# Shared expert tiles load tokens transposed in the attention phase; ScalarE's order within a tile

## The chip, the cores and the metric

The kernel runs on one core of a Trainium2 chip. The metric is device time in microseconds (us) of one execution of the whole program, lower is better. A core has TensorE (PE in the profile), VectorE (DVE), ScalarE (ACT), GpSimd (POOL) and SyncE (SP). They run side by side and wait for each other on semaphores; SP, ACT and POOL also issue DMA transfers.

## The reference

4096 tokens of width 1024 pass through a cross-attention-like product and then through a mixture of experts; each is added to its input:

```python
x = x + einsum("emk,enk->emn", fp8_blocks(layernorm(x)), fp8_blocks(ctx))
h = layernorm(x)                                   # T = 4096 tokens, H = 1024
scores = sigmoid(h @ gate_w)                       # 32 experts; 6 are chosen per token
expert_out = sum_k weight_k * (silu(h @ w_gate[e_k]) * (h @ w_up[e_k])) @ w_down[e_k]   # inner width 704
shared = (silu(h @ sw_gate) * (h @ sw_up)) @ sw_down                                    # inner width 1408
out = x + expert_out + shared
```

## The kernel before

Tokens are handled in tiles of 128. The 4096 tokens are TT = 32 tiles, and the whole program has three stages.

**Attention phase.** For each of the 32 tiles all engines work in a hand-written software pipeline (`beside` of each engine). At its end the normalised tokens of tile i, split into a high and a low float16 part, lie in `x2nat` (128 tokens x 2 x 1024). SP stores them to the DRAM tensor `rows_x` (`store_x2`, L319). TensorE also transposes them into PSUM (`ps_t`), and ScalarE copies them to `xT`, half u = 0 of `xT_pair` (`take_x2`), for the product with the router's matrix (`logits`). SP's loop holds, in order: store of x1, load of the residual, store of x2, load of x for tile i+4, load of ctx for tile i+11. In the last nine tiles parts of the shared expert's weights are loaded too.

**Tiles.** Then follows one loop of tiles, numbered n. Tiles 0 to 31 are all tokens through the first half of the shared expert (704 of its 1408 inner columns). Tiles 32 on are routed tiles: each is 128 token rows of one expert. Here there are 208 of them (tiles 32 to 239), and `n_tiles` is 240. The last 32 tiles are all tokens through the second half of the shared expert. During the first shared pass GpSimd scatters the token rows into the experts' slots in `rows_x` (six indirect DMAs of 512 KB per token tile), and SP loads those tiles for it and writes zeros. During the last pass GpSimd gathers six rows of results per token from `rows_d`, and VectorE adds them (`combine`).

TensorE does, for tile n: gate and up (`gate_up`, 72 matmuls into `ps_gu`), then the down product of tile n-1 (34 matmuls into `ps_d`). The weights are two buffers of an expert each, which GpSimd converts from float32. Before gate and up of tile n it waits for the tokens (`xt_in`) and for `hid` of tile n-1 (`hid_done`), since `ps_gu` is one buffer; before the down product it waits for the transposed hidden values (`ht_in`, tile hT) and for `d_free`.

**ScalarE, per tile** (function `tile`): wait for gate and up of tile n; issue the DMA transposition of the tokens of tile n+2 from `xin` into half u of `xT_pair` (`turn_x`, L907); `silu` (L914); copy VectorE's `hid` to float16 (L920); issue the transposition of the hidden values, `hT` (`turn_h`, L931), once VectorE has written their low part; wait until the tokens of n+2 have landed (`xin_free`) and load those of n+3 into `xin`, which is one buffer (`load_x`, L902); empty `ps_d` of tile n-1 into `dout` (`store_d`, L936) and store that to `rows_d` (L938). In the last shared pass `store_d` is left out, and VectorE takes `ps_d` itself. All of ScalarE's DMAs stand in one queue (q10), all of SP's in another (q1), GpSimd's in a third (q0).

Of the kernel before, what the change touches and what calls it, by code (L numbers as in the profile page):

```python
# [22 lines left out]
F16 = mybir.dt.float16  # L23
# [5 lines left out]
ds = bass.ds  # L29

P = 128
B, S, H = 4, 1024, 1024
# [5 lines left out]
T = B * S  # L38
TT = T // P
# [49 lines left out]
def build(nc, x, ctx_in, gate_w, w_gate, w_up, w_down, sw_gate, sw_up, sw_down, out):  # L89
# [4 lines left out]

    rows_x = nc.dram_tensor("rows_x", (T + SLOT_TILES * P, 2 * H), F16).ap()
    rows_d = nc.dram_tensor("rows_d", (T + SLOT_TILES * P, H), F32).ap()
    rows_x1 = nc.dram_tensor("rows_x1", (T, H), F32).ap()
    last_row = T + SLOT_TILES * P - 1

    with ExitStack() as stack:  # L100
# [6 lines left out]
        def sem(name):  # L107
            return stack.enter_context(nc.semaphore(name))
# [5 lines left out]
        xT_pair = sb("xT", [P, 2, 2 * KH, P], F16)  # L114
# [66 lines left out]
        def pair(area, i):  # L181
# [40 lines left out]
            for n in ("qin_in", "qin_free", "rounded", "unrounded", "deq_ready", "nat_high", "nat_ready"))  # L222
# [13 lines left out]
            sem(n) for n in ("route_step", "top_ready", "sig_ready", "mask_ready", "rank_done", "rank_used",  # L236
                             "slots_ready", "tables_ready", "pad_out"))

        xin_in, xt_in, gu_done, silu_done = (sem(n) for n in ("xin_in", "xt_in", "gu_done", "silu_done"))
        hid_done, hid_high, hid_low, ht_in, down_done, d_free, d_out = (sem(n) for n in (  # L240
            "hid_done", "hid_high", "hid_low", "ht_in", "down_done", "d_free", "d_out"))
# [11 lines left out]
        X, CTX = 0, 1  # L253
# [21 lines left out]
        def set_of_x2(i):  # L275
            return X_SETS - TT + i if isinstance(i, int) and i >= TT - 2 else i * 2 + 3
# [7 lines left out]
        def _(sp):  # L284
# [20 lines left out]
            def load_q(kind, i):  # L305
                sp.wait_ge(qin_free[kind], i + 1)
                sp.dma_start(qin[kind], (x_rows, c_rows)[kind][ds(i * P, P), :]).then_inc(qin_in[kind], 16)
# [9 lines left out]
            def store_x2(i):  # L317
                sp.wait_ge(x2_ready, i + 2)
                sp.dma_start(rows_x[ds(i * P, P), :], x2nat.rearrange("p a d -> p (a d)")).then_inc(x2_out, 16)  # L319

            load_q(CTX, 0)
            load_q(X, 0)
            load_res(0)
# [10 lines left out]
            def stores(i):  # L334
                store_x1(i)
                if not isinstance(i, int) or i < TT - 1:
                    load_res(i + 1)
                store_x2(i)

            with sp.Fori(0, TT - CLEAD - 1) as i:  # L340
                stores(i)
                load_q(X, i + (LEAD + 1))
                load_q(CTX, i + (CLEAD + 1))
            with sp.Fori(TT - CLEAD - 1, TT - CLEAD + 1) as i:
                stores(i)
                load_q(X, i + (LEAD + 1))
            for i in range(TT - CLEAD + 1, TT):
                stores(i)
                if i < TT - LEAD - 1:
                    load_q(X, i + (LEAD + 1))  # L350
                c = STAGES + i - (TT - CLEAD + 1)
                sp.wait_ge(conv_done, c - STAGES + 1)
                load_piece(0, c, *half_a)

            for c in range(STAGES + CLEAD - 1, CHUNKS):
                sp.wait_ge(conv_done, c - STAGES + 1)
                load_piece(0, c, *half_a)
# [431 lines left out]
        def _(act):  # L789
# [9 lines left out]
            def take(high, low, ps):  # L799
                for half, to in enumerate((high, low)):  # L800
                    last = a.activation(to, ps[:, half, :].rearrange("p (k n) -> p k n", k=KH), ACT.Copy)
                return last
# [9 lines left out]

            def take_x2(i):
                act.wait_ge(tr_done, set_of_x2(i) + 1)
                take(xT[:, 0], xT[:, 1], ps_t).then_inc(tr_free, 1)

            def high_of_nat(kind, i):
# [83 lines left out]
            def load_x(n, row):  # L901
                act.dma_start(xin[:, :, :].rearrange("p a d -> p (a d)"), rows_x[ds(row, P), :]).then_inc(xin_in, 16)  # L902

            def turn_x(n, u):
                act.wait_ge(xin_in, n * 16 + 16)
                act.sem_inc(act_turn, 1)
                act.dma_start_transpose(xT_pair[:, u, :, :],  # L907
                                        xin[:, :, :].rearrange("p a d -> p (a d)")).then_inc(xt_in, 16)

            def xin_free(n):  # L910
                act.wait_ge(xt_in, n * 16 + 16)
# [13 lines left out]
            def turn_h(n, u, used=True):  # L925
                act.wait_ge(hid_high, n + 1)
                act.wait_ge(hid_low, n + 1)
                if used:
                    act.wait_ge(down_done, n if n is n_tiles else n - 1)
                act.sem_inc(act_turn, 1)  # L930
                act.dma_start_transpose(hT[:, u, :, :], hid_hl[:, :]).then_inc(ht_in, 16)  # L931
# [5 lines left out]
                act.wait_ge(d_free, n + 2)  # L937
                act.dma_start(rows_d[ds(n * P, P), :], dout[:, :]).then_inc(d_out, 16)  # L938

            def tile(n, u, next_row=None, first=False, turn=True, used=True, store=True):  # L940

                act.wait_ge(gu_done, n + 1)
                if turn:
                    turn_x(n + 2, u)
                silu(n)
                high_of_hidden(n, first)
                turn_h(n, u, used)
                if next_row is not None:
                    xin_free(n + 2)
                    load_x(n + 3, next_row)  # L950
                if store:
                    store_d(n - 1)

            act.wait_ge(x2_out, 16 * TT + 16)
            load_x(0, 0)
            act.wait_ge(logits_done, TT)
            turn_x(0, 0)
            xin_free(0)
            load_x(1, P)
            turn_x(1, 1)  # L960
            xin_free(1)
            load_x(2, 2 * P)
            tile(0, 0, 3 * P, first=True, used=False, store=False)
            tile(1, 1, 4 * P, used=False)
            with act.Fori(1, TT // 2 - 2) as q:
                for u in range(2):
                    tile(q * 2 + u, u, (q * 2 + (u + 3)) * P)
            tile(TT - 4, 0, (TT - 1) * P)

            act.wait_ge(tables_ready, 1)  # L970
            act.wait_ge(pad_out, 16 * E)
            for u in range(2):
                act.wait_ge(scat_out[u], 16 * TOPK * TT // 2)
            tile(TT - 3, 1, TT * P)
            with act.Fori(TT // 2 - 1, N_ALL // 2 - 2) as q:
                for u in range(2):
                    tile(q * 2 + u, u, (q * 2 + (u + 3)) * P)
            tile(N_ALL - 4, 0, (N_ALL - 1) * P)
            n_tiles = act.value_load(count_tab[0:1, 0:1], min_val=N_ALL, max_val=N_MAX)
            act.wait_ge(zeros_out, 16 * (EXTRA + 1))  # L980

            def late(n, u):
                row = act.value_load(row_tab[0:1, ds(n - (N_ALL - 3), 1)], min_val=0, max_val=N_MAX - 1)
                tile(n, u, row * P)

            late(N_ALL - 3, 1)
            late(N_ALL - 2, 0)
# [3 lines left out]
                    for u in range(2):  # L991
                        late(q * 2 + u, u)

            tile(n_tiles, 0, 3 * P)
            tile(n_tiles + 1, 1, 4 * P, store=False)
            with act.Fori(1, TT // 2 - 2) as q:
                for u in range(2):
                    tile(n_tiles + (q * 2 + u), u, (q * 2 + (u + 3)) * P, store=False)
            tile(n_tiles + (TT - 4), 0, (TT - 1) * P, store=False)
            tile(n_tiles + (TT - 3), 1, store=False)  # L1000
            for u in range(2):
                tile(n_tiles + (TT - 2 + u), u, turn=False, store=False)


        @block.vector
# [380 lines left out]
```

## Time and profile before

| | us |
|---|---|
| median of three runs | 7482.79 |
| lowest and highest | 7464.86, 7521.01 |
| the profiled execution, its own time | 7488.26 |
| its span | 7486.6 |
| busy in it: TensorE | 6540.5 (87%) |
| busy: GpSimd | 3376.8 (45%) |
| busy: VectorE | 1598.3 (21%) |
| busy: ScalarE | 1032.4 (14%) |

The page gives shares over the whole span; the stages have different limits, so they are to be read one by one. A DMA share is the mean busy share of the core's 16 DMA engines, and can go over 1 where transfers overlap on an engine. PEclk is TensorE's granted clock, 1.00 being 2.4 GHz.

### The profile page before, as it was taken

What the parts mean: (1) busy time and instruction counts of PE and PEld (TensorE: products, weight loads), DVE (VectorE), ACT (ScalarE), POOL (GpSimd) and SP (SyncE); (2) the same over time, 40 slices, a digit from 0 to 9 for tenths busy, and PEclk for the clock granted to TensorE, in tenths of its full rate; (3) what the DMA queues carried; (4) which work ended last, traced back from release to release, by engine and by line L of the source; (5) the groups of instructions that cost most, each with busy time, mean ns of one, the idle gap of its engine ahead of it and who ended that gap; (6) DMA issues with size and microseconds to landing.
All of it is one profiled execution on the core that took longest, in us unless ns stands there. A gap on an engine that the chain in (4) does not pass through costs nothing.

```text
span 7486.6 us, 89283 instructions
## 1 busy us (share of the span) xinstructions
PE 6540.5 (87%) x32678; PEld 3097.2 (41%) x32679; DVE 1598.3 (21%) x2586; ACT 1032.4 (14%) x1206; POOL 3376.8 (45%) x2190
## 2 busy tenths in 40 slices
PE   1455568768999999999999999999999999988878
PEld 0233333323444444444444444444444444433333
DVE  3555582000011101111110111111011111124435
ACT  1333330000111111111111111111111111100000
POOL 3555584434055336534543564553554545512222
PEclk9777779889999999999999999999999999999989
DMA  1222237997355555555555565555565555567897
GB/s 50 75 84 85 90 128 235 334 294 209 92 154 160 139 138 158 160 141 141 158 153 137 150 170 140 155 162 136 155 168 141 158 154 155 153 191 219 220 199 219
DMA packets 1270964, 1190.42 MB, mean 159 GB/s; under 512 B 995728, under 2 KB 995728, under 8 KB 1270928
## 3 DMA queue, kind: packets, MB, share of 16 engines
q10 hardware_dynamic: 1031168, 509.19, 29.8%
q1 hardware_dynamic: 179856, 471.02, 19.7%
q0 software_dynamic: 59904, 209.75, 8.1%
q8 instruction: 20, 0.33, 0.0%
q14 instruction: 16, 0.13, 0.0%
HBM read 647.10 MB, written 310.38 MB: 128 GB/s over the span
## 4 chain that ended last, share of the span: by engine, by line
PE 73%; DMA 8%; issue 7%; ACTq 5%; POOL 4%; DVE 3%; ACT 1%; SPq 0%; POOLq 0%; DVEq 0%
PE ps_gu L623 50%; PE ps_d L623 20%; ACTq L907 4%; DMA xT<-xin 3%; DMA xin<-rows_x 3%; POOL wts L474 2%; PE ps_d L726 2%; DMA wts<-in_x 2%; PE ps_d L724 1%; ACTq L931 1%; POOL wts L479 1%; DMA hT<-hid_hl 1%; POOL wts L465 0%; DVE hid L1218 0%; DVE amax_p L1032 0%
## 5 line engine op out<-in xcount | busy, mean ns | idle before, releaser
L623 PE MATMUL ps_gu<-wts,xT 128*128 128x512 f16 (+1 forms) x19584 | 3988.4, 366 | 206.5 <-DVE hid L1218 199.2
L623 PEld LDWEIGHTS ps_gu<-wts,xT 128*128 128x128 f16 x19584 | 1908.3, 99 | 2284.6 <-issue 398.4
L623 PE MATMUL ps_d<-wts,hT 128*128 128x512 f16 x8160 | 1829.1, 383 | 119.8 <-DMA hT<-hid_hl 119.3
L449 POOL TENSOR_SCALAR wts<-stage 128x1408 f16<-128x1408 f32 (+1 forms) x476 | 588.5, 1236 | 2422.7 <-PE ps_d L726 2406.2
L1218 DVE SCALAR_TENSOR_TENSOR hid<-ps_gu,sil 128x704 f32<-128x704 f32 x272 | 242.4, 891 | 5083.5 <-ACT sil L914 5083.5
L452 POOL TENSOR_TENSOR wts<-stage,wts 128x1408 f16<-128x1408 f32 (+1 forms) x476 | 1248.2, 2622 | 39.8
L623 PEld LDWEIGHTS ps_d<-wts,hT 128*128 128x128 f16 x8160 | 802.1, 98 | 1090.2 <-DMA hT<-hid_hl 116.3
L914 ACT ACTIVATE sil<-ps_gu 128x704 f32<-128x704 f32 x272 | 205.9, 757 | 4261.6 <-issue 4193.7
L450 POOL TENSOR_SCALAR stage<-stage 128x1408 f32<-128x1408 f32 (+1 forms) x476 | 610.2, 1282 | 0.0
L614 PE MATMUL ps_t<-ident,wts 128*128 128x128 f16 x1024 | 89.0, 257 | 366.2 <-POOL wts L474 361.6
L623 PE MATMUL ps_d<-wts,xin 128*128 128x512 f16 x1536 | 367.6, 399 | 42.4 <-DVE wts L1112 33.0
L936 ACT ACTIVATE dout<-ps_d 128x1024 f32<-128x1024 f32 x240 | 245.6, 1024 | 1088.6 <-issue 530.0
L589 POOL COPY slot_now<-slot 128x6 int32 (+1 forms) x32 | 6.0, 186 | 644.8 <-DVE wts L1250 572.8
L474 POOL TENSOR_TENSOR wts<-wts 128x1024 f16<-128x1024 f32 x64 | 173.7, 2726 | 240.9 <-issue 213.7
L1225 DVE TENSOR_TENSOR hid_hl<-hid,hid_hl 128x640 f16<-128x640 f32 x272 | 265.1, 974 | 0.0
L920 ACT ACTIVATE hid_hl<-hid 128x704 f16<-128x704 f32 x272 | 214.8, 790 | 281.8 <-DVE hid L1218 281.8
L1250 DVE SCALAR_TENSOR_TENSOR wts<-wts,top_w 128x1024 f32<-128x1024 f32 x192 | 246.6, 1284 | 26.4 <-DVE wts L1247 3.6
L623 PEld LDWEIGHTS ps_d<-wts,xin 128*128 128x128 f16 x1536 | 153.2, 102 | 231.7 <-issue 41.5
L614 PEld LDWEIGHTS ps_t<-ident,wts 128*128 128x128 f16 x1024 | 79.1, 117 | 387.1 <-issue 329.0
L594 POOL DMA_INDIRECT wts<-rows_d,slot_now x192 | 192.8, 1004 | 76.9 <-issue 48.8
L553 POOL DMA_INDIRECT rows_x<-wts,slot_now x192 | 186.7, 973 | 78.0 <-issue 49.6
L614 PE MATMUL ps_gu<-ident,wts 128*128 128x128 f16 x512 | 56.3, 299 | 155.3 <-POOL wts L474 155.3
(149 smaller groups left out, 2230.7 us busy)
## 6 DMA issues: line engine op xcount, KB each, us to landing
xin<-rows_x ACTq DMA_DIRECT2D x272, 512.0 KB, 4.0
rows_d<-dout ACTq DMA_DIRECT2D x240, 512.0 KB
stage<-in_L_ffn_w_down SPq DMA_DIRECT2D x384, 256.0 KB, 3.1
stage<-in_L_ffn_w_gate SPq DMA_DIRECT2D x256, 352.0 KB, 3.7
stage<-in_L_ffn_w_up SPq DMA_DIRECT2D x256, 352.0 KB, 4.2
wts<-in_x SPq DMA_DIRECT2D x64, 512.0 KB, 5.6
rows_x<-wts SPq DMA_DIRECT2D x64, 512.0 KB, 3.3
wts<-rows_x SPq DMA_DIRECT2D x64, 512.0 KB, 7.3
```

Of the source, the lines that this page charges most:

```text
L449: g.tensor_scalar(high, raw, WSCALE, 1.0, ALU.mult, ALU.mult).then_inc(conv_step, 1)
L450: g.tensor_scalar(raw, raw, WSCALE, 1.0, ALU.mult, ALU.mult).then_inc(conv_step, 1)
L452: g.tensor_tensor(low, raw, high, ALU.subtract).then_inc(conv_done, 1)
L474: g.tensor_tensor(nat[kind][:, 1, :], deq[kind], nat[kind][:, 0, :], ALU.subtract)\
L614: last = nc.tensor.transpose(to[:, a, k * P:(k + 1) * P], src[:, a, k * P:(k + 1) * P], ident[:, :])
L623: ins = nc.tensor.matmul(dst[c], left, right[c], start=(first and a == 0), stop=(last and a == 2))
L907: act.dma_start_transpose(xT_pair[:, u, :, :], xin[:, :, :].rearrange("p a d -> p (a d)")).then_inc(xt_in, 16)
L920: a.activation(hid_hl[:, 0:M], hid[:, :, :].rearrange("p a c -> p (a c)"), ACT.Copy)\
L936: a.activation(dout[:, :], ps_d_flat, ACT.Copy, scale=1.0 / (WSCALE * HSCALE)).then_inc(d_free, 1)
L1218: v.scalar_tensor_tensor(out=hid[:, :, :].rearrange("p a c -> p (a c)"), in0=ps_gu_flat[:, M:2 * M], scalar=HSCALE / WSCALE, in1=sil[:, :, ...
L1225: v.tensor_tensor(hid_hl[:, M + M_LAST:], flat[:, 0:K_LAST], hid_hl[:, 0:K_LAST], ALU.subtract).then_inc(hid_low, 1)
L1250: ins = v.scalar_tensor_tensor(out=total[u], in0=gat[u][:, k, :], scalar=top_w[:, ds(i, 1), k:k + 1].rearrange("p a k -> p (a k)"), in1=to ...
```

## The change

A new DRAM tensor `cols_x` holds the tokens of each tile in the layout of `xT`. In the attention phase SP stores `xT` of tile i-1 into it once ScalarE has copied it there (`store_xt`), and ScalarE waits for the store of the tile before ahead of the next copy (`take_x2`). In both shared passes ScalarE loads the tokens of tile n+2 from `cols_x` with one plain DMA (`load_t`); `xin` and its transposition remain for the routed tiles. The order in `tile` becomes: `silu`, high part of the hidden values, `turn_h`, then the next tokens (`load_t`, or `turn_x` and `load_x`), then `store_d`.

```diff
+    cols_x = nc.dram_tensor("cols_x", (T, 2 * H), F16).ap()
...
+            def store_xt(i):
+                sp.wait_ge(tr_free, set_of_x2(i) + 2)
+                sp.dma_start(cols_x[ds(i * P, P), :], xT_pair[:, 0, :, :].rearrange("p k n -> p (k n)")).then_inc(xt_out, 16)
...
-            with sp.Fori(0, TT - CLEAD - 1) as i:
+            stores(0)
+            load_q(X, LEAD + 1)
+            load_q(CTX, CLEAD + 1)
+            with sp.Fori(1, TT - CLEAD - 1) as i:
                 stores(i)
                 load_q(X, i + (LEAD + 1))
                 load_q(CTX, i + (CLEAD + 1))
+                store_xt(i - 1)
             with sp.Fori(TT - CLEAD - 1, TT - CLEAD + 1) as i:
                 stores(i)
                 load_q(X, i + (LEAD + 1))
+                store_xt(i - 1)
             for i in range(TT - CLEAD + 1, TT):
                 stores(i)
+                store_xt(i - 1)
                 if i < TT - LEAD - 1:
                     load_q(X, i + (LEAD + 1))
                 c = STAGES + i - (TT - CLEAD + 1)
                 sp.wait_ge(conv_done, c - STAGES + 1)
                 load_piece(0, c, *half_a)
 
+            store_xt(TT - 1)
...
             def take_x2(i):
                 act.wait_ge(tr_done, set_of_x2(i) + 1)
+                if not isinstance(i, int) or i > 0:
+                    act.wait_ge(xt_out, i * 16)
+                    act.sem_inc(act_turn, 1)
                 take(xT[:, 0], xT[:, 1], ps_t).then_inc(tr_free, 1)
...
             def turn_x(n, u):
-                act.wait_ge(xin_in, n * 16 + 16)
+                act.wait_ge(xin_in, (n - TT) * 16 + 16)
...
+            def load_t(n, i, u):
+                if not isinstance(n, int) or n > 0:
+                    act.wait_ge(xt_in, n * 16)
+                act.dma_start(xT_pair[:, u, :, :].rearrange("p k n -> p (k n)"),
+                              cols_x[ds(i * P, P), :]).then_inc(xt_in, 16)
...
-            def tile(n, u, next_row=None, first=False, turn=True, used=True, store=True):
+            def tile(n, u, next_row=None, next_cols=None, first=False, turn=False, used=True, store=True, fresh=False):
 
                 act.wait_ge(gu_done, n + 1)
-                if turn:
-                    turn_x(n + 2, u)
                 silu(n)
                 high_of_hidden(n, first)
                 turn_h(n, u, used)
+                if next_cols is not None:
+                    load_t(n + 2, next_cols, u)
+                if turn:
+                    turn_x(n + 2, u)
                 if next_row is not None:
-                    xin_free(n + 2)
+                    if not fresh:
+                        xin_free(n + 2)
                     load_x(n + 3, next_row)
                 if store:
                     store_d(n - 1)
 
-            act.wait_ge(x2_out, 16 * TT + 16)
-            load_x(0, 0)
+            act.wait_ge(xt_out, 16 * TT)
             act.wait_ge(logits_done, TT)
-            turn_x(0, 0)
-            xin_free(0)
-            load_x(1, P)
-            turn_x(1, 1)
-            xin_free(1)
-            load_x(2, 2 * P)
-            tile(0, 0, 3 * P, first=True, used=False, store=False)
-            tile(1, 1, 4 * P, used=False)
+            load_t(0, 0, 0)
+            load_t(1, 1, 1)
+            tile(0, 0, next_cols=2, first=True, used=False, store=False)
+            tile(1, 1, next_cols=3, used=False)
             with act.Fori(1, TT // 2 - 2) as q:
                 for u in range(2):
-                    tile(q * 2 + u, u, (q * 2 + (u + 3)) * P)
-            tile(TT - 4, 0, (TT - 1) * P)
+                    tile(q * 2 + u, u, next_cols=q * 2 + (u + 2))
+            tile(TT - 4, 0, next_cols=TT - 2)
...
-            tile(TT - 3, 1, TT * P)
+            tile(TT - 3, 1, TT * P, next_cols=TT - 1, fresh=True)
```

The routed tiles get `turn=True` and are called as before; the calls of the last shared pass get `next_cols` in place of a row.

## Rows read from the trace of the kernel before

**Rows 1.** The chain that ended last, on the page: shares of the span by line.

```profile
PE ps_gu L623 50%; PE ps_d L623 20%; ACTq L907 4%; DMA xT<-xin 3%; DMA xin<-rows_x 3%; POOL wts L474 2%; PE ps_d L726 2%; DMA wts<-in_x 2%; PE ps_d L724 1%; ACTq L931 1%; POOL wts L479 1%; DMA hT<-hid_hl 1%; POOL wts L465 0%; DVE hid L1218 0%; DVE amax_p L1032 0%
```

**Rows 2.** Line 914 in three windows: count, ns min/median/max, first and last start.

```profile
L914 ACT ACTIVATE sil<-ps_gu x18: 757/757/757, 1214.7 to 1787.3; 128x704 f32<-128x704 f32 x18
...
L914 ACT ACTIVATE sil<-ps_gu x220: 757/757/761, 1787.3 to 6562.6; 128x704 f32<-128x704 f32 x110
...
L914 ACT ACTIVATE sil<-ps_gu x32: 757/757/757, 6591.1 to 7446.2; 128x704 f32<-128x704 f32 x32
```

**Rows 3.** Windows: length; busy PE, PEld, DVE, ACT, POOL; PEclk, DMA share, GB/s.

```profile
1214.70:1787.30 572.60, 409.43 (x1803) 182.01 (x1801) 31.64 (x51) 43.69 (x51) 230.12 (x247) 0.85 1.06 303
1787.30:6588.60 4801.30, 4797.99 (x23312) 2241.95 (x23311) 512.81 (x660) 565.47 (x660) 2299.84 (x1369) 1.00 0.55 149
6588.60:7446.10 857.50, 718.30 (x3288) 326.22 (x3287) 359.81 (x333) 48.98 (x63) 194.27 (x220) 0.92 0.82 220
```

**Rows 4.** Waits of PE, 1214.7 to 1787.4: total us, times, longest us.

```profile
PE ps_gu L623 <- DVE hid L1218: 93.4, 13, 16.5
PE ps_d L623 <- DMA hT<-hid_hl: 69.2, 7, 18.3
```

**Rows 5.** Waits of PE, 6588.6 to 7446.3.

```profile
PE ps_gu L623 <- DVE hid L1218: 98.7, 21, 10.2
PE ps_d L623 <- DMA hT<-hid_hl: 40.5, 5, 16.4
```

**Rows 6.** Timeline of ACT in a routed tile: start, length, engine, line, operation.

```profile
3028.47 1.88 ACTq L907 DMA_TRANSPOSE xT<-xin  x1
...
3034.07 1.39 ACTq L931 DMA_TRANSPOSE hT<-hid_hl  x1
...
3036.43 1.02 ACT L936 ACTIVATE dout<-ps_d 128x1024 f32<-128x1024 f32 x1 [3.45 <-PE ps_d L726]
```

**Rows 7.** Timeline of ACT, tile 15; in brackets idle before and releaser.

```profile
1600.97 21.39 ACTq L931 DMA_TRANSPOSE hT<-hid_hl  x1
...
1624.55 1.02 ACT L936 ACTIVATE dout<-ps_d 128x1024 f32<-128x1024 f32 x1 [24.66 <-DMA xT<-xin]
```

**Rows 8.** Timeline of PE, the down product of the same tile.

```profile
1631.84 7.94 PE L623 MATMUL ps_d<-wts,hT 128*128 128x512 f16 x30 [18.30 <-DMA hT<-hid_hl]
```

**Rows 9.** Timeline of ACT, tile 0: the turn's issue.

```profile
1145.24 3.77 ACTq L907 DMA_TRANSPOSE xT<-xin  x1
```

**Rows 10.** DMA issues, 1214.7 to 1787.4: count, KB each, median us to landing.

```profile
xin<-rows_x ACTq DMA_DIRECT2D x17, 512.0 KB, 9.3
...
xT<-xin ACTq DMA_TRANSPOSE x17, 20.1
```

**Rows 11.** DMA issues, 6588.6 to 7446.3.

```profile
xin<-rows_x ACTq DMA_DIRECT2D x29, 512.0 KB, 4.0
...
xT<-xin ACTq DMA_TRANSPOSE x30, 14.4
```

**Rows 12.** Timeline of the last tile: hT's issue and its use.

```profile
7449.79 4.60 ACTq L931 DMA_TRANSPOSE hT<-hid_hl  x1
...
7463.14 8.97 PE L623 MATMUL ps_d<-wts,hT 128*128 128x512 f16 x30 [9.54 <-DMA hT<-hid_hl]
```

**Rows 13.** Timeline of SP's queue in the attention phase.

```profile
592.25 0.45 SPq L307 DMA_DIRECT2D wts<-in_ctx  x1
...
1084.86 0.34 SPq L319 DMA_DIRECT2D rows_x<-wts  x1
```

**Rows 14.** DMA issues, 300 to 900, attention phase.

```profile
wts<-in_ctx SPq DMA_DIRECT2D x19, 512.0 KB, 6.2
```

**Rows 15.** Timeline of ACT: xT copies of a steady step and of tile 31.

```profile
604.07 1.91 ACT L801 ACTIVATE xT<-ps_t 128x1024 f16<-128x1024 f16 x2
...
1086.81 1.94 ACT L801 ACTIVATE xT<-ps_t 128x1024 f16<-128x1024 f16 x2 [4.18 <-PE ps_t L614]
```

**Rows 16.** Timeline of POOL: its last operation on the first routed expert's weights.

```profile
1823.87 2.13 POOL L452 TENSOR_TENSOR wts<-stage,wts 128x1024 f16<-128x1024 f32 x1
```

## What I predict

> **What bounds the kernel now.** I read the page's chain first: TensorE's two products hold 70% of it, but a transposition's issue on ScalarE's queue, the transpositions `xT<-xin` and the loads `xin<-rows_x` hold 10% more [rows 1]. The next question is in which stage. The counts of `silu` give the stages in tiles [rows 2]: tile 3 at 1214.7 us, tile 20 at 1787.3, tile 239 at 6562.6, and 32 more, the second shared pass, up to 7446.2. The 219 steps of the middle take 4775.3 us, 21.81 us each, and TensorE is busy in 4798.0 of 4801.3 us there at full clock [rows 3]: that is the time of a tile when nothing disturbs it. Against it the two shared passes are slow:
>
> - Tiles 3 to 20, while GpSimd scatters the rows and the DMA share is 1.06: 572.6 us for 17 steps, 33.7 each. At 21.81 they would be 370.7, so 201.9 us are lost. TensorE was idle for 572.6 - 409.4 = 163.2 of them; the other 38.7 are matmuls at a granted clock of 0.85 [rows 3].
> - The second shared pass, while GpSimd gathers, DMA share 0.82: 857.5 us for 31 steps, 27.7 each. At 21.81 that is 676.1, so 181.4 are lost: 139.2 idle, 42.2 clock [rows 3].
>
> Together 383 us are there to be had. TensorE's waits say on what it idles: on `hid` 93.4 us in 13 waits and on `hT` 69.2 in 7 [rows 4]; in the second pass on `hid` 98.7 in 21 and on `hT` 40.5 in 5 [rows 5]. `hid` itself is cheap. In a quiet tile ScalarE issues xT's transposition (1.88 us), `silu` follows, and hT is issued 5.60 us after the start of the turn [rows 6]; TensorE has the down product of the tile before to do meanwhile and sees nothing of it. In the crowded stretches the issue of a transposition takes up to 21.39 us [rows 7] and xT's stands ahead of `silu`: gate and up of the next tile wait for `hid`. hT is then queued behind xT, and the down product waits for it: issued at 1600.97, used at 1631.84, 30.9 us later [rows 7, 8]. ScalarE also stands 24.66 us before it empties `ps_d`, because `xin_free` waits for xT to land [rows 7]. xin is a single buffer: load, turn, load follow each other whatever TensorE does.
>
> **The change, part by part.** *First tile.* The issue of 3.77 us stood between the product and `silu` with TensorE idle [rows 9]; it goes: 3.8 us gained.
>
> *Shared tiles, order.* `silu` and the copy come first, then hT is issued: by the quiet tile 5.60 - 1.88 = 3.7 us after the product ends. The slow issue can no longer delay `hid`, so the waits on it of 93.4 and 98.7 us go, unless ScalarE is late for another reason: after hT it has one plain load to issue and, in the first pass, `dout` to make and store, due 21.8 us after the product.
>
> *Shared tiles, transfers.* xT's 16 blocks of 128x128 per tile are no longer transposed, hT's 11 are. A plain load of the same 512 KB landed in 9.3 us where the transposition took 20.1 [rows 10]. The wait in `xin_free`, and the turn that depends on a load, go too. So what is late next is hT alone. It may take 21.8 - 3.7 = 18.1 us. Its price with nothing of xT ahead is seen once, in the last tile with a gather running: issued at 7449.79, used at 7463.14, 13.4 us [rows 12]. In the scatter stretch xT's 20.1 scaled by 11/16 gives 13.8. Both fit into 18.1; the tail doesn't, the late one above took 30.9 with xT ahead. I take one tile in three of the scatter stretch 4 us late, with 2 us of slow clock behind each stall (38.7 / 17 = 2.3 per tile now): 2.0 us a tile. In the gather stretch, where transposition and load land in 14.4 and 4.0 us [rows 11], I take 0.8. Bounds: nothing, and on the other side 6 us in each tile of the first and 3 in each of the second (hT at about 22 us in every tile of the first pass, between 13.8 and 30.9).
>
> Of the 572.6 us I keep 490 as crowded (the last step is quiet already, and the scatter should end some 50 us sooner with the small packets gone; 50 us more or less are only 50 x 2.0 / 23.8 = 4 us of the sum). 490 / 23.8 = 20.6 tiles, 41 us lost instead of 201.9: 161 gained. In the second pass 31 x 0.8 = 25 us instead of 181.4: 156 gained. VectorE, which combines there, is busy 359.8 / 31 = 11.6 us a tile [rows 3] and is no new bound.
>
> The Trainium skill (Advanced Engine Details and Errata, X-Bar Transpose) says that on trn2 a transposing DMA is as fast as a regular one. In the scatter stretch it isn't: 20.1 against 9.3 us [rows 10]. By the rule only one of two equal passes over the tokens would be saved, and I would halve the part of the gain that comes from transfers.
>
> *Routed tiles.* Nothing is removed; the turn moves behind hT. xT then lands behind hT's issue at 3.7 us, two issues of 1.4 and 1.9 us and both transfers, at about 11 us (estimate: 3.7 + 3.3 + 4). ScalarE stands in `xin_free` until then; queued behind it are the next load and `dout`, which starts at 7.96 us now [rows 6] and would at about 12. TensorE needs `ps_d` at 21.8, so there are 9 us of cover: cost 0.
>
> *Attention phase.* A store of 512 KB per tile goes on SP's queue. In a steady step it follows the load of ctx, issued at 592.25, so near 592.7 [rows 13]. That load lands 6.2 us after its issue [rows 14], the store then near 600; ScalarE's new wait stands ahead of the xT copies at 604.07 [rows 15]. 4 us of cover, 0 paid. In five of the last nine steps the store stands ahead of the load of x: 0.5 us on each, 2.5. At the very end it is seen: the store of tile 30 goes out behind the one at 1084.86 [rows 13], lands near 1090 (estimate, a little under the 6.2), and the copy of tile 31 starts now at 1086.81 [rows 15]: 3.3 us on the path to the routing. Together 6 (bounds 0 and 20, the latter one us in each of twenty steps).
>
> *The first routed weights.* Tile 23.6 would be at 1214.7 + 490 = 1705 and tile 31 at 1866; tile 32's product follows the down product. GpSimd ends its last part of these weights at 1826 [rows 16]: 40 us of cover, 0 paid, unless the scatter ends that much later than now.
>
> Sum: 7486.6 - 3.8 - 161 - 156 + 6 = 7172 of span. The profiled execution took 7488.3, 1.7 more than its span and 5.5 more than the median shown, so against the median 7168; I say **7170 us**.
>
> **Rivals.** *(a) hT takes the place of both.* It moves slowly among scatter and stage traffic even with nothing ahead of it, because of its many small packets. At the bounds above: 490 / 27.8 = 17.6 tiles x 6 = 106 and 31 x 3 = 93 us lost, so 383.3 + 3.8 - 199 - 6 = 182 gained, 7301 us. For it: seven waits on hT, up to 18.3 us [rows 4]. Against: xT was ahead in all of them, and the 13.4 us seen alone [rows 12]. The Trainium skill (DMA: Bandwidth & Descriptors, Queues, rings and completion order) has each DMA engine go round between its queues packet by packet; that rule speaks for this rival, as small packets would then give way to large ones as often.
>
> *(b) No change.* The DMA engines are full, they stay full, and what is left waits as long as before; within 1%. Against: in the second pass their share is 0.82 [rows 3], so there is room, and the `hid` waits are of order, not of bytes.
>
> *(c) Slower: the routed tiles.* If xT behind hT lands after some 20 us, `dout` comes too late and each of the 208 routed tiles stretches. The point is 9 us beyond my 11; 1.5 us a tile beyond that eat the whole gain, and 2 give 416 - 315 = +101, 7584 us. Against: at the middle's DMA share of 0.55 [rows 3] ScalarE's plain loads land in 4 us or so, as they do at 0.82 [rows 11].
>
> **How the numbers follow.** Forecast 0.74, (a) 0.18, (b) 0.04, (c) 0.04. The forecast's own range is 7115 (both stretches nearly clean) to 7260. The range reaches up to (a): 7110 to 7300. Over 1% is about what can be told from no change here. Faster than that are the forecast, (a) and a little of the rest: 0.93; same 0.03; slower 0.04.
>
> **What would show it.** In the changed profile: steps of `silu` of 23 to 24 us in the scatter stretch and near 22.6 in the second pass; waits on `hid` all but gone, those on hT fewer but not zero; granted clock above 0.95 in both; full TensorE in the routed tiles; tile 3 at most 5 us later than now. Steps of 27 and 25 us with hT as the releaser would make (a) right. If `hid` is still waited for, the order was not the cause. Gaps ahead of the routed tiles' down products would be (c). A first product more than 20 us later would make my cost of the attention phase wrong.

## The result and the profile after

| | before | after |
|---|---|---|
| median, us | 7484.82 (4 runs) | 7118.26 (4 runs) |
| lowest and highest | 7464.86, 7521.01 | 7109.32, 7169.77 |
| ratio, with 95% interval | 1 | 0.9519 [0.9461, 0.9578] |
| span of the profiled execution | 7486.6 | 7113.4 |

The changed kernel is 4.8% faster. It was run again on another chip with some of the experiments below: 7126.09 us (7119.70 to 7140.62) against 7586.19 (7502.76 to 7629.47) for the kernel before there, 0.9425 [0.9354, 0.9496]. All ratios in this document leave out executions that took over 1.5% longer than the fastest of their kernel on that chip; medians and ranges hold them.

The lines of `silu` (L936 now; line numbers are those of the changed kernel) answer to [rows 2], in the same three parts, tiles 3 to 20, 20 to 239, 240 to 271:

```profile
L936 ACT ACTIVATE sil<-ps_gu x18: 757/757/757, 1202.8 to 1582.4; 128x704 f32<-128x704 f32 x18
...
L936 ACT ACTIVATE sil<-ps_gu x220: 757/757/757, 1582.4 to 6362.0; 128x704 f32<-128x704 f32 x110
...
L936 ACT ACTIVATE sil<-ps_gu x32: 757/757/757, 6388.8 to 7074.7; 128x704 f32<-128x704 f32 x32
```

The scatter stretch takes 379.6 us for its 17 steps (22.3 each, it was 33.7), the second pass 685.9 for 31 (22.1 each, it was 27.6 by this count). The middle has not moved. The windows with the same ends, to be read against [rows 3]:

```profile
1202.80:1582.40 379.60, 372.89 (x1803) 173.68 (x1802) 31.50 (x51) 43.67 (x51) 156.22 (x181) 1.00 1.01 328
1582.40:6362.00 4779.60, 4776.05 (x23216) 2234.41 (x23215) 532.12 (x657) 562.94 (x658) 2382.01 (x1441) 1.00 0.58 156
6388.80:7074.70 685.90, 678.15 (x3288) 316.62 (x3287) 361.97 (x333) 49.00 (x64) 201.25 (x220) 1.00 0.82 253
```

TensorE is idle 6.7 us in the first stretch (it was 163.2) and 7.8 in the last (139.2, in a window 2.4 us longer), and the granted clock is 1.00 in both. The DMA share has hardly moved, 1.01 and 0.82, but it now goes with 328 and 253 GB/s in place of 303 and 220. Waits of TensorE, first in the scatter stretch and then in the second pass; these are all that are left of [rows 4, 5], and none is on `hid`:

```profile
PE ps_d L636 <- DMA hT<-hid_hl: 6.7, 3, 2.4
...
PE ps_d L636 <- DMA hT<-hid_hl: 7.7, 2, 7.1
```

ScalarE in one tile of the scatter stretch, which answers to [rows 7]. hT's issue is still slow, but `silu` is ahead of it, and behind it stands a load of 1.60 us:

```profile
1337.85 0.76 ACT L936 ACTIVATE sil<-ps_gu 128x704 f32<-128x704 f32 x1 [12.82 <-PE ps_gu L636]
...
1341.52 6.70 ACTq L953 DMA_TRANSPOSE hT<-hid_hl  x1
1348.48 1.60 ACTq L929 DMA_DIRECT2D xT<-cols_x  x1
1350.21 1.02 ACT L958 ACTIVATE dout<-ps_d 128x1024 f32<-128x1024 f32 x1 [9.77 <-issue]
```

On the page's chain TensorE's two products are at 77% (70% in [rows 1]), and neither the transposition of the tokens nor their load is among its entries; hT's transposition is still there with 2%:

```profile
PE ps_gu L636 53%; PE ps_d L636 24%; POOL wts L487 2%; PE ps_d L739 2%; DMA hT<-hid_hl 2%; DMA wts<-in_x 2%; PE ps_d L737 2%; POOL wts L492 1%; POOL wts L478 0%; DVE amax_p L1050 0%; DVE stats_q L1108 0%; DVE wts L1284 0%; POOL wts L480 0%; SPq L321 0%; ACT wts L843 0%
```

### The profile page after: what moved, and what is told of

Its sections match the earlier page's. It is cut to its first block, busy times and chain, and to the rows that moved or that the text cites. A ratio compares the mean times of both kernels' runs of the same rounds, so it can differ in the third digit from the quotient of the medians.

```text
span 7113.4 us, 89519 instructions
## 1 busy us (share of the span) xinstructions
PE 6460.4 (91%) x32678; PEld 3079.8 (43%) x32679; DVE 1619.6 (23%) x2586; ACT 1032.1 (15%) x1206; POOL 3385.2 (48%) x2190
## 4 chain that ended last, share of the span: by engine, by line
PE 81%; issue 8%; DMA 4%; POOL 4%; DVE 3%; ACT 0%; SPq 0%; POOLq 0%; ACTq 0%; DVEq 0%
PE ps_gu L636 53%; PE ps_d L636 24%; POOL wts L487 2%; PE ps_d L739 2%; DMA hT<-hid_hl 2%; DMA wts<-in_x 2%; PE ps_d L737 2%; POOL wts L492 1%; POOL wts L478 0%; DVE amax_p L1050 0%; DVE stats_q L1108 0%; DVE wts L1284 0%; POOL wts L480 0%; SPq L321 0%; ACT wts L843 0%
## 5 line engine op out<-in xcount | busy, mean ns | idle before, releaser
L636 PE MATMUL ps_gu<-wts,xT 128*128 128x512 f16 (+1 forms) x19584 | 3929.7, 362 | 9.2 <-DVEq L1324 4.0
L636 PE MATMUL ps_d<-wts,hT 128*128 128x512 f16 x8160 | 1810.5, 380 | 26.8 <-DMA hT<-hid_hl 26.8
L465 POOL TENSOR_TENSOR wts<-stage,wts 128x1408 f16<-128x1408 f32 (+1 forms) x476 | 1232.2, 2589 | 39.8
L463 POOL TENSOR_SCALAR stage<-stage 128x1408 f32<-128x1408 f32 (+1 forms) x476 | 628.6, 1321 | 0.0
L936 ACT ACTIVATE sil<-ps_gu 128x704 f32<-128x704 f32 x272 | 205.9, 757 | 2844.8 <-PE ps_gu L636 2514.1
L636 PE MATMUL ps_d<-wts,xin 128*128 128x512 f16 x1536 | 368.7, 400 | 44.4 <-DVE wts L1130 34.2
L1243 DVE TENSOR_TENSOR hid_hl<-hid,hid_hl 128x640 f16<-128x640 f32 x272 | 299.6, 1102 | 0.0
```

The source lines that it names most:

```text
L463: g.tensor_scalar(raw, raw, WSCALE, 1.0, ALU.mult, ALU.mult).then_inc(conv_step, 1)
L465: g.tensor_tensor(low, raw, high, ALU.subtract).then_inc(conv_done, 1)
L636: ins = nc.tensor.matmul(dst[c], left, right[c], start=(first and a == 0), stop=(last and a == 2))
L936: a.activation(sil[:, :, :].rearrange("p a c -> p (a c)"), ps_gu_flat[:, 0:M], ACT.Silu, scale=1.0 / WSCALE).then_inc(silu_done, 1)
L1243: v.tensor_tensor(hid_hl[:, M + M_LAST:], flat[:, 0:K_LAST], hid_hl[:, 0:K_LAST], ALU.subtract).then_inc(hid_low, 1)
```

## The experiments

Two things were changed in the shared tiles at once: what is transferred (a plain load for load, turn and wait) and in which order ScalarE issues it. Theory A is that the transposition's traffic and the chain through xin were the cost, theory B that the slow issue ahead of `silu` was. Two kernels do one of the two each, which with the kernel before and the changed one makes a table of four.

### The order alone

```diff
# kernel before, tile()
-                if turn:
-                    turn_x(n + 2, u)
                 silu(n)
                 high_of_hidden(n, first)
                 turn_h(n, u, used)
+                if turn:
+                    turn_x(n + 2, u)
```

> The kernel before with one part of the change: silu, the high part and hT's issue come first in every tile, the turn of the next tokens after them; tokens still go through xin and are transposed in every tile. Theory A (the transposition and the single xin buffer are the cost): in the crowded stretches ScalarE's queue has to do hT (9.8 us), xT (20.1) and the load (9.3) one after the other, 39 us, so the steps of tiles 3 to 20 stay at 33 us or more; in the second shared pass 10.6 + 13.7 + 4.0 = 28, so steps near 28; the total stays above 7420 us. Theory B (the order is the cost, because a slow issue stood ahead of silu): steps of 22 to 24 us in both, total 7120 to 7180 us.

Measured: 7261.41 us (7254.95 to 7262.57), 0.9556 [0.9489, 0.9624]. Its windows, scatter stretch and second pass:

```profile
1206.10:1734.30 528.20, 402.19 (x1804) 179.32 (x1803) 31.49 (x51) 43.73 (x52) 208.02 (x240) 0.88 1.03 323
6538.50:7215.70 677.20, 676.28 (x3289) 316.29 (x3287) 362.08 (x333) 49.04 (x64) 201.97 (x220) 1.00 0.90 278
```

Neither theory has the total right (over 7420, and 7120 to 7180), because each fits one pass. In the second, theory B holds: the order alone takes all, 677.2 us, 21.8 per step, with every token tile still transposed. In the scatter stretch a step is 31.1 us, nearer to theory A's 33 than to B's 22 to 24, and the wait has moved. The waits of ScalarE and of TensorE there:

```profile
ACT dout L936 <- DMA xT<-xin: 443.5, 17, 39.3
...
PE ps_d L623 <- ACT dout L936: 120.4, 14, 22.9
```

Nothing waits for `hid` any more. ScalarE stands in `xin_free` before it may empty `ps_d`, and TensorE waits for that.

### The plain loads alone

```diff
# changed kernel, tile()
+                if next_cols is not None:
+                    load_t(n + 2, next_cols, u)
+                if turn:
+                    turn_x(n + 2, u)
                 silu(n)
                 high_of_hidden(n, first)
                 turn_h(n, u, used)
-                if next_cols is not None:
-                    load_t(n + 2, next_cols, u)
-                if turn:
-                    turn_x(n + 2, u)
```

> The changed kernel with the old order in every tile: the next tokens (plain load in shared tiles, turn in routed tiles) are issued ahead of silu. Theory A (transposition and xin are the cost): a plain load is issued in 0.4 to 1.6 us and puts only 128 rows ahead of hT; steps of 22 to 23 us in both shared passes, total 7118 to 7170 us. Theory B (the order is the cost): waits of TensorE on hid come back, steps of 27 us or more, total above 7300 us.

Measured: 7162.69 us (7120.72 to 7212.69), 0.9446 [0.9357, 0.9535].

```profile
1207.00:1595.40 388.40, 375.07 (x1804) 174.05 (x1803) 31.52 (x51) 43.74 (x52) 151.99 (x175) 0.98 1.03 314
6408.90:7084.50 675.60, 675.60 (x3286) 316.16 (x3285) 362.28 (x333) 49.01 (x64) 195.42 (x220) 1.00 0.78 257
```

22.8 us a step in the scatter stretch, 21.8 in the second pass: theory A's numbers in both. So in the first pass what is transferred gives nearly all of the gain without the order (184 of 193 us in the table), and the order without it does not (31.1 us a step). In the second, order and transfers each suffice, and neither may be credited with the gain by itself. "What is transferred" is still three things at once: the packets, the chain through xin, and the length of the issue, since a plain load is issued in a short time wherever it stands. Reckoned from profiled executions in us, for 17 and 31 steps:

| | scatter stretch | second pass |
|---|---|---|
| before, first chip | 572.6 | 855.1 |
| order alone | 528.2 | 677.2 |
| plain loads alone | 388.4 | 675.6 |
| both (the change), first chip | 379.6 | 685.9 |
| both, another chip | 384.4 | 686.5 |

The first column has to be read with care. The rows of order alone and of plain loads alone are from a chip on which the kernel before took 7516 to 7634 us and was not profiled. By the medians there the order alone is 336 us faster (7597.41 to 7261.41), while the table gives it 44.4 + 177.9. The difference is not located, and the scatter stretch also took 519.3 us in a kernel further down (less gather) that is the kernel before up to there. What the order alone gives in the scatter stretch is therefore not shown: somewhere from nothing to about 160 us. That 31.1 us a step are left with it, and 22.8 with the plain loads, is.

### The transposition's packets with nothing that depends on them

```diff
# changed kernel, tile(): 14 of xT's 16 blocks, zeros into a buffer that nobody reads
                 if next_cols is not None:
                     load_t(n + 2, next_cols, u)
+                    extra_turn(next_cols - 2 + extra_base[0])
...
+            def extra_turn(count):
+                if not isinstance(count, int) or count > 0:
+                    act.wait_ge(extra_in, count * 16)
+                act.sem_inc(act_turn, 1)
+                act.dma_start_transpose(spare_to[:, :, :], spare_from[:, :]).then_inc(extra_in, 16)
```

> The changed kernel, and in every shared tile that loads tokens ScalarE also issues, behind the plain load, a transposition of 14 blocks (xT has 16) from a buffer of zeros into a buffer that nobody reads; the only wait is for the one of the tile before. So the transposition's packets are back in the queue, but nothing depends on them: no bounce through xin, no xin_free, silu still first. If the packets themselves are the cost: hT has to go behind what is left of them, about 9.8 + 17.5 = 27 us in the scatter stretch and 10.6 + 12 = 23 in the second pass, steps of 28 to 33 us for tiles 3 to 20 and 24 to 27 in the second pass, total near 7400 us. If the chain load, turn, load and the waits on it are the cost: steps of 22 to 24 us, total below 7170 us.

Measured: 7373.38 us in one run. Windows as before:

```profile
1203.40:1806.50 603.10, 404.94 (x1804) 179.90 (x1803) 31.58 (x51) 43.71 (x51) 186.04 (x217) 0.83 1.10 251
6655.50:7331.60 676.10, 676.10 (x3288) 316.28 (x3286) 362.08 (x333) 48.98 (x64) 201.00 (x220) 1.00 0.89 277
```

In the scatter stretch the extra transposition alone brings the slow pass back, 35.5 us a step, with no chain through xin. The total is what was expected of the packets, but by other terms: the second pass does not suffer at all (24 to 27 us a step were expected), another 43 us stand in tiles 20 to 32 (308.2 against 265.6 in the change), where GpSimd issues its last scatter at 1875 in place of 1699, and in the scatter stretch TensorE hardly waits for hT. It waits for `dout`, which stands behind the issue of the extra transposition:

```profile
1513.48 19.96 ACTq L942 DMA_TRANSPOSE spare_to<-spare_from  x1
1533.57 1.02 ACT L970 ACTIVATE dout<-ps_d 128x1024 f32<-128x1024 f32 x1 [31.31 <-DMA xT<-cols_x]
...
PE ps_d L640 <- ACT dout L970: 185.8, 12, 23.7
...
PE ps_d L640 <- DMA hT<-hid_hl: 8.0, 2, 4.7
```

This edit also put the slow issue ahead of `dout`, so it shows that a second transposition per tile suffices for slow steps, and not whether by its packets or by its issue. The next kernel has `dout` ahead of everything slow.

### The turn behind everything

```diff
# kernel before, tile()
-                if turn:
-                    turn_x(n + 2, u)
                 silu(n)
                 high_of_hidden(n, first)
                 turn_h(n, u, used)
+                if store:
+                    store_d(n - 1)
+                if turn:
+                    turn_x(n + 2, u)
                 if next_row is not None:
                     xin_free(n + 2)
                     load_x(n + 3, next_row)
-                if store:
-                    store_d(n - 1)
```

> The kernel before with silu, hT and dout first in every tile and the turn and the load of the next tokens last; nothing is stored in the attention phase. In the order-only kernel TensorE's waits in the scatter stretch had moved to dout (120.4 us in 14 waits), which stood behind the wait for xT. If that place was all that was wrong, steps of 22 to 24 us for tiles 3 to 20 and a total near 7130 us: the stores and plain loads would not be needed. If the transposition's traffic is the cost there, ScalarE is then late for the next silu instead, because hT (15 us), turn (14 to 30) and load don't fit into 21.8: waits on hid or hT come back, steps of 27 us or more for tiles 3 to 20, total 7200 to 7300 us; the second pass is at 21.8 either way.

Measured: 7313.88 us (7279.63 to 7384.13), 0.9652 [0.9571, 0.9733]. In the profiled execution (span 7382.4, the upper end) the scatter stretch takes 656.5 us, 38.6 a step, at 260 GB/s and a share of 1.09; the second pass again 676.1. Waits of TensorE and of ScalarE in the stretch:

```profile
PE ps_gu L623 <- DVE hid L1218: 137.9, 12, 21.6
PE ps_d L623 <- DMA hT<-hid_hl: 91.0, 14, 11.7
...
ACT sil L914 <- DMA xT<-xin: 355.9, 11, 45.2
```

With the turn ahead of `silu` the wait is on `hid` and hT, behind hT it is on `dout`, behind `dout` it is on `hid` and hT again. None of the three places in ScalarE's queue helps in the scatter stretch. In the order-alone kernel it takes 20.4 us in the median from hT's issue to xT's last packet, and hT is issued 3.7 us after the product ends; with the turn last it takes 32.2. With the 3.7 us both are over the 21.8 us of a tile, and `xin_free` makes ScalarE wait for the end of it. Two things were not tried: a second xin buffer, with which ScalarE need not stand in `xin_free` (355.9 us ahead of `silu` above), and the turn on an engine other than ScalarE. How much of the cost is traffic and how much is this waiting stays open. From the packet records of ScalarE's queue, the time from an issue to the end of its last packet, median and longest, in us (order of the packets taken as that of the issues):

```
in us                     hT            xT
scatter stretch
before                  12.7, 29.5    20.1, 26.1
order alone             15.2, 27.8    13.7, 33.1
turn last               18.3, 23.7    25.3, 40.4
plain loads alone       11.8, 24.8    -
the change               9.8, 19.9    -

second pass
before                   3.1, 27.3    13.7, 29.2
order alone             10.5, 17.1     6.7, 14.7
the change              10.6, 22.0    -
```

The lower part shows why order alone is enough in the second pass. Before, the turn met the gather (13.7 us) while `silu` waited behind it, and hT came when the gather was over (3.1): in the 4 us after an issue the gather's packets fill 0.51 of the DMA engines' time in the median for xT and nothing for hT. With hT first, hT meets the gather (0.46) and takes 10.5 us, for which there are 18.1, and the turn comes behind it and takes 6.7.

### Less gather

```diff
# kernel before, gather() and combine()
-                for k in range(TOPK):
+                for k in range(1):
                     g.indirect_dma_start(
...
-                dve.wait_ge(gat_in[u], pair * (16 * TOPK) + 16 * TOPK)
+                dve.wait_ge(gat_in[u], pair * 16 + 16)
```

> The kernel before with one of the six gathers per tile in the last shared pass; VectorE still adds six rows, five of which are left-over data, so the output leaves out part of the routed experts' sum. Tokens are still transposed, ahead of silu. If the cost in the second pass is the meeting of the slow turn with the gather's traffic, the issue of the turn is short there again (1.4 to 2 us) and the steps are 21.8 to 22.5 us, 31 of them 676 to 697 us instead of 855. If the transposition or the order cost by themselves, steps stay at 27 us or more. The first shared pass is as slow as before in either case.

Measured: 7249.38 us in one run, beside 7516.76 for the kernel before. The second pass takes 683.4 us (first `silu` 6533.06, last 7216.49), 22.0 a step, and TensorE's waits on `hid` there are down from [rows 5]:

```profile
PE ps_gu L623 <- DVE hid L1218: 8.2, 10, 1.7
```

So neither order nor transposition costs anything there by itself. It takes the whole gather. The issue of the turn did not become as short as expected: 4.1 us in the median and up to 7.06, where 1.4 to 2 were expected and 9.5 was the median before. With issues of that length TensorE waits no more than the 8.2 us above.

### What the stores in the attention phase cost

```diff
# kernel before, with store_xt, its place on SP's queue and the wait in take_x2, as in the change; and
             act.wait_ge(logits_done, TT)
+            act.wait_ge(xt_out, 16 * TT)
             turn_x(0, 0)
```

> The kernel before with the attention phase's part of the change alone: the stores of xT to cols_x and ScalarE's waits for them; cols_x is not read, shared tiles load and turn as before. By the prediction's term the first product of tile 0 starts 6 us later than the 1128.7 us of before (bounds 0 and 20), so at 1135, and the total is 7491 us. The rival, from the changed kernel's own trace (first product at about 1126.5): the stores cost nothing that shows, start within 3 us of 1128.7, total within 0.3% of before.

Measured: 7592.04 us (7486.58 to 7633.76) beside 7597.41 (7516.30 to 7633.94) on that chip, 0.9898 [0.9793, 1.0003]. That can't tell 6 us from nothing. From its profile only the start of the first product is read, here beside two other kernels:

```profile
1129.58 16.74 PE L636 MATMUL ps_gu<-wts,xT 128*128 128x512 f16 x72 [3.99 <-DVEq L1323]
...
1129.65 16.55 PE L623 MATMUL ps_gu<-wts,xT 128*128 128x512 f16 x72 [3.99 <-DVEq L1306]
...
1126.24 16.60 PE L636 MATMUL ps_gu<-wts,xT 128*128 128x512 f16 x72 [3.98 <-DVEq L1324]
```

These are stores alone, order alone (no stores) and the change. With stores and the change's order on SP's queue it starts at 1126.2 to 1129.6 in six profiles, without stores at 1127.7 (less gather), 1128.7 (before), 1129.7 (order alone) and 1135.3 (turn last). The stores cost nothing that can be seen against that spread.

### The old place of the turn in routed tiles

```diff
# changed kernel, tile(); next_cols stays where it is
+                if turn:
+                    turn_x(n + 2, u)
                 silu(n)
                 high_of_hidden(n, first)
                 turn_h(n, u, used)
                 if next_cols is not None:
                     load_t(n + 2, next_cols, u)
-                if turn:
-                    turn_x(n + 2, u)
```

> The changed kernel with the old place of the turn in the routed tiles alone (ahead of silu). By the prediction the later turn costs nothing, because dout has some 9 us of cover: ScalarE's wait for xT ahead of dout (1953 us in 209 waits in the changed kernel) should all but go, and the total should be the same within 0.3%, 7110 to 7170 us. If the cover does not hold, this is faster by 20 us or more.

Measured: 7143.91 us (7132.29 to 7170.44) beside 7126.09 for the change. ScalarE's waits for xT ahead of `dout` went from 1953.1 us to 4.5, and tiles 32 to 239 took 4513.5 us against 4514.0 in the change: the wait was wholly covered. The 18 us of difference in the medians are not explained by the edit, which touches no tile before 30. In the profiled executions the difference is 32 us, and it stands between tiles 20 and 32 (301.4 us against 263.4), where the scatter ran until 1765 instead of 1705:

```profile
PE ps_gu L636 <- POOLq L586: 9.8, 1, 9.8
```

TensorE waited 9.8 us for the first routed expert's weights, and 16.8 in there for hT. In the change GpSimd's last part of them starts at 1786.09, and tile 32's first product starts at 1833.52, some 45 us later; in this execution the last part started at 1865.46. The cover that I put at 40 us had gone there.

### Loads of x ahead of the store of x2

Left after the change is the attention phase, in which VectorE waits 204.0 us in 22 waits for the load of x. SP issues it behind the store of x2, which waits for GpSimd.

```diff
# changed kernel, SP's queue, tiles 0 to 22
+            def store_1(i):
+                store_x1(i)
+                load_res(i + 1)
...
-                stores(i)
+                store_1(i)
                 load_q(X, i + (LEAD + 1))
                 load_q(CTX, i + (CLEAD + 1))
+                store_x2(i)
                 store_xt(i - 1)
```

> The changed kernel, and on SP's queue in the attention phase the loads of x for tile i+4 and of ctx for tile i+11 stand ahead of the store of x2 of tile i instead of behind it (tiles 0 to 22); the rest is the same. In the changed kernel VectorE waits 204.0 us in 22 waits for the load of x, up to 9.6 us each, because SP first waits for GpSimd's last operation of the step. If that order is the cause, these waits go, a steady step shortens from 31.4 us to 25 to 28, the first product starts 70 to 130 us earlier and the total is 6990 to 7060 us. The rival: GpSimd or VectorE is the bound right behind it and the step stays above 30 us, total within 20 us of the changed kernel's.

Measured: 7097.32 us (7089.08 to 7101.62), below every run of the changed kernel on that chip (7119.70 to 7140.62); against the kernel before 0.9377 [0.9308, 0.9447]. The first product starts at 1099.63 instead of 1128.50, 28.9 us earlier, where 70 to 130 were expected; a steady step takes 29.9 us instead of 31.2. The wait on the load is gone and another has come in its place:

```profile
DVE safe L1079 <- POOL amax L479: 191.4, 23, 8.7
DVE scale_l L1145 <- ACT std_l L854: 83.2, 23, 3.9
```

VectorE now waits for GpSimd's maximum over the partitions (107.8 us in the change). So the rival was nearly right: what VectorE waits for right behind the load is GpSimd. It is still the fastest version here.

## Why the prediction was right, and where its sizes were off

7170 us was predicted, 7118 measured, inside 7110 to 7300. On the profiled executions the sum said 314.8 us of gain and 373.2 came: 11.9 up to tile 3 (-2.2 forecast), 193.0 in the scatter stretch (161), 169.2 in the second pass (156), and 0.9 lost in the rest. All three terms were too cautious, and the sum stays inside the range because that reaches to 7110. By its steps:

- **The time of an undisturbed tile, 21.81 us**, held in every kernel, and as the floor of both passes.
- **First tiles: 3.8 us gained for the turn, 6 lost in the attention phase, so +2.2; measured -11.9 at tile 3.** The turn went as said, and the first product came 2.4 us earlier instead of 6 later. With the turn went what I had not counted: the loading of ScalarE's table (1.28 us) now stands behind the first loads at 1099.10, far ahead of the first product, and tile 0's `silu` starts 16.6 us after its product instead of 21.7. The same holds for tiles 1 to 3, whose `silu` is no longer behind a turn of 1.8 to 2.5 us.
- **The attention phase, 6 us, was wrong in its larger term.** The wait that I named came at the end: ScalarE stood 6.3 us for the store of tile 30 ahead of the copy of tile 31.

```profile
1086.45 1.94 ACT L814 ACTIVATE xT<-ps_t 128x1024 f16<-128x1024 f16 x2 [6.26 <-DMA cols_x<-xT]
```

  Yet the copy starts at 1086.45, before 1086.81 of [rows 15], because the steps ahead of it ended earlier; SP's store of tile 31 stands at 1082.42 against 1084.86. One wait is not one loss while phases differ by as much between executions.
- **The scatter stretch** is where the sum was furthest off. The 41 us were for 20.6 tiles, up to the end of the scatter; in tiles 3 to 20 8.9 us are left over the undisturbed time (379.6 - 370.7) and in tiles 20 to 32 another 3.9, so 12.8. The mis-sized term is the late tail of hT. I took one tile in three 4 us late, without a row that showed either figure, and 2 us of slow clock behind it. Three tiles of 17 were late, with waits of at most 2.4 us, and the clock stayed at 1.00. The allowance of 18.1 us was right: by the packet records just three hT took longer (19.0, 19.1 and 19.9 us). The price, 13.8 us by scaling xT's 20.1 with 11/16, was too high as well: 9.8 in the median. In the kernel before hT took 12.7, near that proportion, so the 20.1 were themselves a price of the old traffic. The scatter ended 38 us sooner (its last issue at 1699 instead of 1737), where I had 50.
- **The second pass: 25 us left, 9.8 were** (685.9 - 676.1). All of it falls on the first steps, where the gather starts; 29 of the 31 steps are 21.8. hT took 10.6 us in the median where 13.4 had been read from one tile, and up to 22.0, once over the 18.1.
- **`hid` and the order.** "The slow issue can no longer delay `hid`" is true, and in the second pass it is enough. In the scatter stretch it is not: order alone leaves 528.2 us, as the 120.4 us of waits on `dout` show. My text gave the order the `hid` waits of both passes; in the first pass they turn into waits on `dout`. The total could hold all the same because both were changed together; the prediction never asked what either does alone.
- **The routed tiles, 0,** held: `dout` waits 1953.1 us for xT in 209 waits, 9.3 each, and starts 10.5 us after `silu` where I had about 12. TensorE does not notice. Rival (c) is ruled out.
- **Rival (a)**, hT in the place of both, was not there: 14.4 us of waits on hT in both passes. The rival had hT at 22 us in every tile of the scatter stretch; it took 9.8 in the median. **Rival (b)** was right that the DMA share stays where it was and wrong that the waits stay with it: the share hardly changed (1.06 to 1.01) while TensorE went from 71.5% busy to 98%. A share of 1 says that the engines have work, not that what is asked of them is late.
- **The rule of the Trainium skill** (Advanced Engine Details and Errata, X-Bar Transpose), that a transposing DMA is as fast as a regular one, would have halved the gain from transfers. In a quiet routed tile the records agree with it: 3.8 us to xT's last packet and 4.3 to its landing, about the 4.0 to the landing of a load of as many bytes. Among other traffic they don't: a share of 1.10 moved 251 GB/s with the extra transpositions, 1.01 moved 328 without.

The scatter stretch also differs most between executions: with two transpositions per tile it took 519 to 657 us in five profiles, with hT's alone 380 to 392 in five. What sets a step to 24 or to 56 us in the kernel before was not tried apart.

## What to carry to other kernels

A DMA whose issue can be slow belongs on an engine's queue behind everything that somebody is waiting for, and where no place in the queue is free of waiters, the transfer itself has to become cheaper: here by storing once what was otherwise transposed twice. When two edits are made at once, take them apart stage by stage, since one can be all of the gain in one stage and needless in the next. The cover of a moved wait is worth as much as the slowest execution leaves of it.

## What the runs showed of the hardware

- The issue of a DMA transposition occupies ScalarE for 1.3 to 29.5 us, with the order of the kernel before up to 21.4. In quiet routed tiles of that kernel it is 1.3 to 2.8 us for either of the two, in its scatter stretch 6.4 us for hT and 9.2 for xT in the median. Plain loads of as many bytes were issued in 0.4 to 1.8 us in the changed kernel's scatter stretch, but single ones took 3.8 in its second pass and 5.6 in the scatter stretch of the kernel before.
- VectorE's subtraction for hT took 2.00 us, and the short one ahead of it 2.91, in a tile during which GpSimd converted weights; the usual times are 0.82 and 0.2. hT's issue moves back by up to 4 us in such tiles. In the changed kernel 66 of the 272 subtractions of 128x640 took 1.65 to 2.00 us, and all 66 overlap one of GpSimd's TENSOR_SCALAR operations on the weights; the 125 during which GpSimd did nothing took at most 0.82. Taking GpSimd's work away was not tried.

```profile
1719.20 2.91 DVE L1242 TENSOR_TENSOR hid_hl<-hid,hid_hl 128x64 f16<-128x64 f32 x1 [0.94 <-ACT hid_hl L942]
1722.04 2.00 DVE L1243 TENSOR_TENSOR hid_hl<-hid,hid_hl 128x640 f16<-128x640 f32 x1
```
